# A transformer layer on one core: the order of helper work in its first stage is changed

## Time and profile before

| | before |
|---|---|
| median of three runs | 1362.12 us |
| the profiled execution | 1367.17 us |
| its span, first to last instruction | 1365.4 us |
| TensorE matmul busy | 1296.0 us, 95% |
| VectorE busy | 1061.4 us, 78% |
| ScalarE busy | 915.4 us, 67% |
| GpSimd busy | 959.2 us, 70% |
| mean granted TensorE clock | 0.988 |
| first stage | 0 to 310 us |

### The profile page before, as it was taken

How to read it: one execution, slowest core, us unless ns; L and a number is a source line. 1 busy time by engine, 2 the same in 40 slices (tenths; PEclk the granted TensorE clock), 3 DMA queues, 4 the chain that set the end, 5 groups by cost and what they waited for, 6 DMA issues and landing times.

```text
span 1365.4 us, 33237 instructions
## 1 busy us (share of the span) xinstructions
PE 1296.0 (95%) x11838; PEld 832.1 (61%) x11838; DVE 1061.4 (78%) x2856; ACT 915.4 (67%) x1752; POOL 959.2 (70%) x1304
## 2 busy tenths in 40 slices
PE   3899999998999999999999999999999999999988
PEld 2444444445666666676666767676767666666754
DVE  7767786887878778787878787878878787878753
ACT  3322322227878888787878788887878787878851
POOL 1322222206888888898888888898989888888853
PEclk9999999998999999999999999999999999999998
DMA  7489899543212121132323131322222232313121
GB/s 258 119 229 271 218 246 231 156 148 93 66 33 64 38 74 49 48 79 58 91 51 87 40 87 49 87 54 82 56 72 78 53 93 54 87 41 87 48 63 62
DMA packets 170870, 133.13 MB, mean 97 GB/s; under 512 B 81554, under 2 KB 139154, under 8 KB 170706
## 3 DMA queue, kind: packets, MB, share of 16 engines
q1 hardware_dynamic: 149042, 113.96, 31.2%
q10 hardware_dynamic: 21664, 17.05, 4.7%
HBM read 74.86 MB, written 42.21 MB: 86 GB/s over the span
## 4 chain that ended last, share of the span: by engine, by line
PE 64%; DVE 6%; ACT 3%; issue 2%; POOL 1%; DMA 0%; ACTq 0%; SPq 0%; DVEq 0%
PE bank L1344 20%; PE bank L1358 12%; PE bank L1322 9%; PE bank L179 8%; PE bank L1309 8%; PE bank L1375 6%; DVE ga L1246 1%; ACT th L1143 1%; DVE junk L202 1%; DVE mx L207 1%; ACT p L1166 1%; DVE probs L987 1%; POOL probs L987 1%; DVE fu L1251 1%; ACT probs L1136 1%
## 5 line engine op out<-in xcount | busy, mean ns | idle before, releaser
L1166 ACT ACTIVATE p<-bank,s_exp 128x512 f32<-128x512 f32 x576 | 395.8, 687 | 188.6 <-PE bank L1309 180.7
L987 POOL TENSOR_TENSOR probs<-p,probs 128x512 f16<-128x512 f32 x448 | 514.0, 1158 | 1.1 <-ACT probs L1136 1.1
L1136 ACT CAST probs<-p 128x512 f16<-128x512 f32 x576 | 351.8, 611 | 0.1
L1096 POOL TENSOR_SCALAR_AFFINE_SELECT p<-p 128x256 f32<-128x256 f32 (+1 forms) x320 | 152.8, 478 | 127.8 <-ACT p L1166 127.7
L207 DVE TENSOR_REDUCE mx<-bank 128x1 f32<-128x512 f32 x264 | 180.2, 686 | 74.7 <-PE bank L179 69.9
L179 PE MATMUL bank<-k_st,q_st 96*128 96x512 f16 (+3 forms) x792 | 221.6, 328 | 15.0 <-DVE mx L207 9.2
L1322 PEld LDWEIGHTS bank<-v_sb,probs 128*128 128x128 f16 x4608 | 198.1, 97 | 51.7 <-issue 1.6
L1309 PE MATMUL bank<-q_st,k_st 98*128 98x512 f16 (+3 forms) x768 | 221.2, 329 | 6.2 <-PEq L254 4.6
L1322 PE MATMUL bank<-v_sb,probs 128*128 128x65 f16 x4608 | 213.9, 192 | 2.7 <-DVE attn L1213 2.7
L1344 PE MATMUL bank<-xt,wg 128*128 128x256 f16 x1536 | 200.2, 273 | 6.3 <-DVE fu L1251 5.5
L1344 PE MATMUL bank<-xt,wu 128*128 128x256 f16 x1536 | 200.1, 273 | 0.0
(11 more groups left out here) (114 smaller groups left out, 1560.9 us busy)
## 6 DMA issues: line engine op xcount, KB each, us to landing
q_st<-q_parts SPq DMA_DIRECT2D x201, 64.0 KB, 2.1
k_st<-k_parts SPq DMA_DIRECT2D x201, 64.0 KB, 2.0
v_sb<-v_parts SPq DMA_DIRECT2D x66, 132.0 KB, 2.2
xt<-xn_parts SPq DMA_DIRECT2D x17, 512.0 KB, 4.5
v_parts<-res SPq DMA_DIRECT2D x8, 1056.0 KB, 6.7
xn_parts<-x_t SPq DMA_DIRECT2D x16, 512.0 KB, 7.7
q_parts<-qk_st SPq DMA_DIRECT2D x32, 256.0 KB, 4.5
k_parts<-qk_st SPq DMA_DIRECT2D x32, 256.0 KB, 4.2
```

The source lines that it names most:

```text
L987: ops.tensor_tensor(probs[s % 2][:, LO, at], p32[k % RING][:, :], probs[s % 2][:, HI, at], ALU.subtract).then_inc(signal, 1)
L1096: nc.gpsimd.affine_select(out=at, in_=at, compare_op=ALU.is_ge, fill=0.0, base=0, pattern=[[0, blocks], [1, P]], channel_multiplier=-1).th ...
L1136: nc.scalar.copy(probs[s % 2][:, HI, u * 512:(u + 1) * 512], p32[k % RING][:, :]).then_inc(p_hi, 1)
L1166: nc.scalar.activation(p32[k % RING][:, :], st_bank[(s + u) % 2][:, :], ACT.Exp, scale=s_exp[:, :]).then_inc(exp_done, 1)
```

## The change

- The bounds of weights 1 and 2: weight 1 is spread in bank 0 instead of 2, behind group 0 instead of ahead of it; weight 2's maximum is taken ahead of tile 0, its power right after the low part of weight 1, its spread behind group 2. Its high part is made after group 3 and it is copied at group 6. VectorE copies its pieces of weight 1 ahead of group 2.
- Statistics of x(t+2) are taken in tile t after group 10, and x(t+1) is normalised after group 0 of tile t; high part, load and transposes are two groups earlier.
- Loads and rounding of the ffn parts move to other slots, the heads' loads to the first group of tiles 3, 4 and 5.
- The bound of the ffn is spread after group 8 of tile 7, its maxima at group 4 and its factors at group 9.
- `xt` and the output buffers share memory with the first raw weight (`shared`), and SP loads the first `xt` at group 5 of tile 7. The constant rows of the fourth k buffer are set by GpSimd.

```diff
-WEIGHTS_SPLIT = {(0, 2): (2,), (3, 6): (3,)}
-WEIGHTS_COPIED = {(0, 3): (1,), (0, 5): (2,), (5, 8): (3,)}
-WMAX_SPREAD = {(0, 1): 2, (3, 3): 3}
-X_TURNED = {5: 0, 7: 1}
+WEIGHTS_SPLIT = {(0, 3): (2,), (3, 6): (3,)}
+WEIGHTS_COPIED_DVE = {(0, 2): (1,), (0, 6): (2,), (5, 8): (3,)}
+WEIGHTS_COPIED = {(0, 3): (1,), (0, 6): (2,), (5, 8): (3,)}
+WMAX_SPREAD = {(0, 0): 1, (0, 2): 2, (3, 3): 3}
+X_TURNED = {3: 0, 5: 1}
...
-FF_LOADED = {(1, 0): ((0, 1), (1, 1)),
-             **{(t, 6): ((2, t),) for t in range(1, NT - 1)},
-             **{(t, 8): ((0, t + 1),) for t in range(1, NT - 1)},
-             **{(t + 1, 0): ((1, t + 1),) for t in range(1, NT - 1)}, (NT - 1, 4): ((2, NT - 1),)}
-X_LOADED = {**{(t, 4): t + 2 for t in range(1, NT - 2)}, (0, 7): 2}
+FF_LOADED = {(1, 0): ((0, 1), (1, 1)), (1, 5): ((2, 1),), (1, 7): ((0, 2),), (1, 10): ((1, 2),), (2, 0): ((2, 2),),
+             **{(t, 6): ((0, t + 1),) for t in range(2, NT - 1)},
+             **{(t, 8): ((1, t + 1),) for t in range(2, NT - 1)},
+             **{(t + 1, 0): ((2, t + 1),) for t in range(2, NT - 1)}}
+X_LOADED = {**{(t, 2): t + 2 for t in range(1, NT - 2)}, (0, 7): 2}
...
-HEADS_LOADED = {(2, 3): 0, (2, 6): 1, (3, 3): 2}
+HEADS_LOADED = {(3, 0): 0, (4, 0): 1, (5, 0): 2}
...
+                    if (t, c) == (NT - 1, 5):
+
+                        sp.wait_ge(xt_stored, 16 * 2 * NT)
+                        sp.wait_ge(w_hi_done, 4)
+                        sp.wait_ge(w_lo_done, 4)
+                        sp.dma_start(keep["shared"][:, 0:KC * FT].bitcast(F16).rearrange("p (k t) -> p k t", t=FT),
+                                     xn_dram[0:1].rearrange("a p w k t -> p (a w k) t")).then_inc(keep["xt_loaded"], 16)
...
-            return bank[(2, 2, 5, 0)[m]][:, 0:P]
+            return bank[(2, 0, 5, 0)[m]][:, 0:P]
...
-                    if c == (7 if t == 0 else 4) and has_next(t):
+                    if c == (7 if t == 0 else 2) and has_next(t):
                         x_high(t + 1)
...
             weights_max(1)
             weights_power(1)
+            weights_max(2)
...
-            first_tile = {0: ("max 2",), 1: ("power 2",), 2: ("statistics",), 3: ("low 2",), 4: ("normalise",),
-                          6: ("magnitude 0",), 7: ("add 0",), 8: ("off 0", "magnitude 1"), 9: ("add 1",), 11: ("off 1",)}
-            last_tile = {0: ("magnitude 20", "add 20"), 1: ("off 20",), 2: ("magnitude 21",), 3: ("add 21",),
-                         4: ("off 21", "magnitude 22"), 5: ("add 22",), 6: ("off 22",), 7: ("magnitude 23", "add 23"),
-                         8: ("off 23",), 9: ("maxima",), 11: ("factors",)}
+            first_tile = {3: ("statistics 1",), 4: ("low 2",), 5: ("normalise 1",),
+                          6: ("magnitude 0",), 7: ("add 0",), 8: ("off 0", "magnitude 1"), 9: ("add 1",),
+                          11: ("off 1", "statistics 2")}
+            second_tile = {0: ("normalise 2",), 1: ("magnitude 2",), 2: ("add 2",), 3: ("off 2", "magnitude 3"),
+                           4: ("add 3",), 5: ("off 3",), 6: ("magnitude 4",), 7: ("add 4",), 8: ("off 4", "magnitude 5"),
+                           9: ("add 5",), 10: ("statistics 3",), 11: ("off 5",)}
+            last_tile = {0: ("magnitude 21", "add 21"), 1: ("off 21",), 2: ("magnitude 22",), 3: ("add 22",),
+                         4: ("off 22", "maxima"), 5: ("magnitude 23", "add 23"), 6: ("off 23",), 9: ("factors",)}
...
-                return {0: ("statistics",), 1: ("magnitude " + a,), 2: ("normalise",), 3: ("add " + a,),
+                later = (f"statistics {t + 2}",) if t + 2 < NT else ()
+                return {0: (f"normalise {t + 1}",), 1: ("magnitude " + a,), 3: ("add " + a,),
                         4: ("off " + a, "magnitude " + b), 5: ("add " + b,) + w3.get((t, 5), ()), 6: ("off " + b,),
                         7: ("magnitude " + c,), 8: ("add " + c,), 9: ("off " + c,),
-                        11: w3.get((t, 11), ())}
+                        10: later, 11: w3.get((t, 11), ())}
...
                     if t == c == 0:
                         weights_low(1)
+                        weights_power(2)
...
             turn_first_x()
-            spread_max(1)
...
-                    if t == 0 and c in (0, 3):
-
-                        pe.wait_ge(wpow_set, 2 + c // 3)
+                    if t == 0 and c == 3:
+
+                        pe.wait_ge(wpow_set, 3)
...
+                    if (t, c) == (NT - 1, 8):
+                        spread_ff_maxima()
...
-        xt = sb("xt", [P, 2, KC, FT], F16)
+        xt = keep["shared"][:, 0:KC * FT].bitcast(F16).rearrange("p (w k t) -> p w k t", w=2, k=KC)
...
-            load_tile(0)
...
+            nc.gpsimd.memset(k_st[3][3 * DK:3 * DK + 2, :], MSCALE).then_inc(ones_set, 1)
...
-            nc.vector.memset(k_st[3][3 * DK:3 * DK + 2, :], MSCALE).then_inc(ones_set, 1)
```

More of the change, by code:

```diff
@@ L259, in sem @@
             return ctx.enter_context(nc.semaphore(name))
-        w_raw = [sb(f"w_raw{m}", [P, KC, D], F32) for m in range(3)]
+        w_raw = [keep["shared"][:, :].rearrange("p (k d) -> p k d", k=KC)]
+        w_raw += [sb(f"w_raw{m}", [P, KC, D], F32) for m in (1, 2)]
         w_part = [sb(f"w_part{i}", [P, 2, KC, D], F16) for i in range(2)]
@@ L748, in plan_of @@
             def plan_of(t):
-                if t in (0, NT - 1):
-                    return last_tile if t else first_tile
-                a, b, c = (f"{3 * t - 1 + i}" for i in range(3))
+                if t in (0, 1, NT - 1):
+                    return {0: first_tile, 1: second_tile, NT - 1: last_tile}[t]
+                a, b, c = (f"{3 * t + i}" for i in range(3))
                 w3 = {(2, 11): ("max 3",), (3, 5): ("power 3",), (4, 11): ("low 3",)}
-                return {0: ("statistics",), 1: ("magnitude " + a,), 2: ("normalise",), 3: ("add " + a,),
+                later = (f"statistics {t + 2}",) if t + 2 < NT else ()
@@ L760, in tile @@
                 for c in range(12):
-                    for m in WEIGHTS_COPIED.get((t, c), ()):
+                    for m in WEIGHTS_COPIED_DVE.get((t, c), ()):
                         copy_weights(m)
@@ L793, in tile @@
                             take_step_off(int(m))
-                        elif has_next(t):
-                            {"statistics": norm_statistics, "normalise": normalise}[name](t + 1)
+                        elif name == "statistics":
+                            norm_statistics(int(m))
+                        elif name == "normalise":
+                            normalise(int(m))
                     if t >= NT - 2:
@@ L839, in spread_max, with spread_ff_maxima @@
                 nc.tensor.matmul(wmax_bank(m), ones[:, :], spread[:, m, :], start=True, stop=True).then_inc(wmax_mm, 1)
+            def spread_ff_maxima():
+                pe.wait_ge(rows.m_red, NM + (NM - 1) // len(early_banks) * len(early_banks) + 1)
+                pe.wait_ge(ffspread, 1)
+                nc.tensor.matmul(bank[0][:, :], ones[:, :], spread[:, :, :].rearrange("p n q -> p (n q)"), start=True,
+                                 stop=True).then_inc(ffmax_mm, 1)
             pe.wait_ge(ident_set, 1)
@@ L935, in attend @@
         res = keep["res"]
-        o_sb = [sb(f"o_sb{i}", [P, D], F32) for i in range(2)]
+        o_sb = [keep["shared"][:, KC * FT + i * D:KC * FT + (i + 1) * D] for i in range(2)]
         st_bank, m_bank = bank[0:2], bank[2:4]
@@ L943, in attend @@
         q_loaded, v_loaded, row_loaded, mt_copied = rows.q_loaded, rows.v_loaded, rows.row_loaded, rows.mt_copied
-        xt_loaded = sem("xt_loaded")
+        xt_loaded = keep["xt_loaded"]
         xb_loaded = sem("xb_loaded")
@@ L1068, in _ @@
             pool.sem_inc(res_done, 1)
+            nc.gpsimd.memset(k_st[3][3 * DK:3 * DK + 2, :], MSCALE).then_inc(ones_set, 1)
+            pool.wait_ge(ones_set, 1)
             def add_down(i, t):
@@ L1490, in build @@
                 "c_ff": sb("c_ff", [P, FC], F32), "ds_row": sb("ds_row", [P, D], F32),
-                "res": sb("res", [P, QB, D], F32), "v_stored": sem("v_stored")}
+                "res": sb("res", [P, QB, D], F32), "v_stored": sem("v_stored"),
+                "shared": sb("shared", [P, KC * D], F32), "xt_loaded": sem("xt_loaded")}
         rows = Rows()
```

## The result

The changed kernel takes 1352.76 us, the median of five runs (1350.97 to 1353.96), beside 1362.42 for the kernel before (five runs, 1360.91 to 1368.0): a ratio of 0.9918 (of the means), 95% interval 0.9895 to 0.9942. By the medians it is faster by 9.7 us, half of the 20 that were predicted, and outside the predicted range of 1336 to 1351. The profiled execution took 1353.43, with a span of 1351.7.

A forecast was written before the change was run, and what follows sets the result against it. The prediction took the first stage as the bound, with TensorE waiting for late x and losing clock. Terms 6.7 + 9.7 + 2.7 + 0.85 = 19.95 us took 1367.17 to 1347.2, or 1342 for the median; range 1336 to 1351.

The forecast's parts named there:

- Tile 5 is tighter ... Hidden, by 1.5 us: Tile 5: x's high part queues behind the scales' loads; even an 11.4 us landing, at T+31.5, precedes tile end T+33.0.
- The sign of being wrong that came true: First stage: the prediction is wrong if TensorE waits inside tiles for VectorE's low parts; no size given.
- Tile 0, 6.7 us: Tile 0's reordered weight bounds and statistics: tile 1 starts at 61.0 instead of 67.67, still set by x; 6.7 us.
- a rival at 1 to 2 us: VectorE's rounding delays x's low part 1 to 2 us per tile; sum 17 to 18 us instead of 20.
- Tiles 1 to 7, 9.7 us: x made a tile ahead: waits at tiles 3, 5 and 6 go, with half clock after two; 9.7 us.
- The end, 2.7 us: End of first stage: ffn maxima and factors earlier, so attention starts sooner after V's store; 2.7 us (2.3 to 2.9).
- The first x, 0.85 us: Start of attention: its first x is loaded some 20 us sooner, in tile 7, so TensorE's wait goes; 0.85 us.
- slower: Attention's 3072 matmuls at L1344 read x from shared memory; at 10 ns more each, 1373 us; chance 0.03.
- Clock kept: Tile 1 and start of attention: clock stays full after shorter gaps, 1.6 + 3 us more, 1337 us; chance 0.10.
- Some waits for x stay: Tile 6 and one more keep 2 to 3 us waits and half clock, 6 to 8 us back, 1349; chance 0.15.
- faster by over 0.5%: Whole kernel: more than 6.8 us faster, covering the forecast, kept clock, staying waits and half of "little"; chance 0.93.

The follow-up runs named there:

- b: Changed kernel with the scales' loads issued ahead of the x load after group 2 of tile 5; 1349.89 us.
- c: Changed kernel with the loads of head 2 at the start of tile 6 instead of tile 5; 1352.35 us.
- e: Changed kernel with the high part of tile 6's x made after group 3 of tile 5 instead of group 2; 1352.15 us.
- a: Changed kernel with the scales' loads issued after group 4 of tile 6 instead of group 2 of tile 5; 1347.7 us.
- n: Kernel h with tile 0's order of weights, statistics and normalising as before the change; 1349.25 us.
- h: Kernel a with tile 0's high part of the next x after group 6 instead of 7, its transpose ahead of group 7's store; 1344.21 us.
- g: Kernel a leaving out the rounding of the first two ffn weight parts, but for 8 columns of one step; 1344.08 us in one run.
- d: The kernel before the change, unedited, profiled a second time; 1361.73 us.
- f: The kernel before with only the heads' loads moved to the start of tiles 3, 4 and 5; 1357.6 us.
- i: Kernel h with ffn maxima and factors at their old groups and attention's first x loaded in attention; 1346.92 us.
- k: Kernel h with x's load, high part and transposes at their old groups, statistics and heads' loads left as changed; 1354.59 us.

## Why the prediction was wrong

The step that failed is "Tile 5 is tighter ... Hidden, by 1.5 us". Its first error is a length. With T the tile's start (188.68), it took the scales' issues at their old length behind 0.4 us of x load, so ScalarE would be free at about T+12.3; it was free at T+19.3 (207.99 - 188.68). Of the 7.0 us, 1.9 are the x load's wait for the normalising, which the prediction had itself at T+9.5 and did not put ahead of the load, and 5.1 are the issues, 9.05 us instead of 3.91 with 1 MB before them in the queue. b and c show that it was the x load's place and not the head's loads.

The second error is the path. The prediction followed x's chain alone behind the issues: queued behind the same issues, and behind the high part of x, was the emptying of group 3, which TensorE wanted first. The prediction had named this rule itself, for VectorE (four banks, 2.8 us of cover), and not applied it to ScalarE. With the length that it assumed this would have cost nothing: the high part ends at T+14.3, emptying and low part of group 3 (0.6 and 0.7) at T+15.6, and group 7 wants the bank at T+18.1 (seven groups of 2.59). With the real length it became a wait, 1.9 us of which are the high part's place by run e. Cost: 4.37 us of wait and 2.4 of half clock in the profile, 4 to 5 us by the medians. Without it (run a) the time, 1347.7, lies within the predicted range. The sign of being wrong that came true is the last one named, TensorE waiting inside a tile for VectorE's low part.

The Trainium skill, "DMA: Bandwidth & Descriptors", section "Issuing engines are not separate DMA queues", says that the time a sequencer spends to initiate a DMA is usually small beside the DMA. Here it was not: 5.25 us of issue, for 256 KB that had landed 8.5 us after the issue began.

The other steps:

- *Tile 0, 6.7 us.* Right in mechanism, too large: tile 1 starts 5.0 us sooner from profile to profile (67.67 to 62.63; 68.92 in the second profile of before), and by 5.3 from n to h. The wait for the bound and the half clock of group 0 went, but group 0 started at 23.08, not 22.2 (x's own transposes took 3.11 us instead of 2.41, and 0.83 of waiting followed), and x's low part took 6.69 us, not 5.6. The prediction priced such a block by VectorE as a rival at 1 to 2 us; g, with most of VectorE's steps beside it gone, makes it 1.46 shorter. But the steps alone do not set the price: in the changed kernel the low part took 6.69, 6.25 and 5.54 us in tiles 0, 2 and 3, each time beside the same two steps (1.8 and 1.31 us), which began 0.6, 1.6 and 2.7 us after it. Nor are the steps new beside it, as the prediction has it: in the old order it took 6.5 to 6.6 us beside such steps in tiles 1 to 5. The rule of the Trainium skill, "SBUF — State Buffer", section "Who interferes with whom", fits these numbers; no run here has the low part with no two-input step beside it.
- *Tiles 1 to 7, 9.7 us.* The waits at 3, 5 and 6 went; without the new wait (run a), from tile 1's start to attention's first matmul took 229.3 us, against 243.1 and 240.6 in the two profiles of before. That is 11.3 to 13.9, where the two terms, x's slots and the end, made 12.4. But 3.3 us of the 9.7 were in the first profile only (tile 6, run d). f shows 3.5 us of it to be the heads' move alone. One term was put at nothing without a reason: the issue of the first transposing DMA, which held SyncE for 4.7, 8.0, 4.5 and 4.1 us in tiles 1 to 4. In tiles 2 to 4 the second was issued at T+21.2 to T+22.6, not T+17.3, and in tile 2 the spare time was all but gone, as the last section shows.
- *The end, 2.7 us.* The gap fell from 4.56 to 2.53, 2.0 us: the start came 1.14 after the store of V, not 0.55.
- *The first x, 0.85 us.* No wait for it is left. But that wait differs from run to run in the old order (0.85, 1.23 in run d, 0.50 in f), and i, with the load in attention, waited only 0.34 and was, 15 score matmuls in, 0.5 us further on than h, counted from attention's start: the granted clock was back at 1.00 some 6.5 us after that start in i and 8.4 in h. In sum with the end, i is 0.7 to 2.7 us slower than h, not clear of noise.
- *The base.* One profiled execution was taken for the kernel. By the second one the tile starts held 6.8 us and not 9.7 (3.59 + 1.7 + 0.44 + 1.03), and 2.6 us of attention were the first's alone; the shift to the median could not set the first right, since the gain was subtracted whole. From the first profile to that of the changed kernel, attention's start moved by 11.7 us (310.81 to 299.13), where 19.1 were forecast for it. The 7.4 that are missing are 6.7 (tile 5), 1.7 (tile 0) and 0.7 (the end), less 1.7 gained that was not forecast: 1.0 at the row maxima in tile 6, for which TensorE waited 1.18 us in three places before and 0.17 after, and 0.7 that was not traced.
- *Two readings.* The one slice of the page below full that is not the last is the tenth, 307 to 341 us: it is the gap between the stages and the start of attention, and no slice of the first stage shows the lost clock. And the chances given for "faster by over 0.5%" add up to 0.94, not 0.93.

Of the rivals, "slower" found nothing: the matmuls that read `xt` from shared memory take 272 to 273 ns each, 272 before. "Clock kept" did not come true in the changed kernel (2.85 us of wait at tile 1) but does in g and h, at 1.41 and 1.29. "Some waits for x stay" named a time, 1349, that is nearer to the measured one than the forecast, but not for its reason: in the changed kernel's profile no tile from 2 to 7 starts late.

What stays open: why single transposes take 13 to 15 us to land, and whether that is why runs of one kernel differ by 3 us and more.

## What to carry to other kernels

Before a transfer's issue is moved, write down everything behind it on the engine that issues it, and take its length from what will stand ahead of it in the queue, not from the old trace. A wait seen in one profile is worth its length only if a second profile has it too. And slack put before a DMA should be counted against the longest landing seen and from when its queue is really free: here 2.4 us were left over the longest landing (T+28.7 against T+31.1), and 0.1 us remained of them in tile 2, since the DMA was issued 5.3 us later than forecast.

## What the runs showed of the hardware

The same transposing DMA landed after 4.2 to 15.0 us. In the first profile of the kernel before, two of whose landings are in the earlier trace rows, 12 of 14 took 4.2 to 6.8 us; in the changed kernel tile 2's took 11.9 and 8.4, and the last landed at 126.4, when tile 3 started at 126.46. A shorter distance to x's load alone does not explain it: in tile 2 that load was issued 4.9 us before the first transpose, 6.0 in the kernel before, but 7.1 in k's tile 1, where they took 12.4 and 15.0.

TensorE's granted clock stayed at 1.00, which is 2.4 GHz, after waits of 1.29, 1.41, 1.63 (n, tile 6) and 1.68 us. At 2.2 us it went both ways: 0.50, which is 1.2 GHz, in the 3 us after the 2.21 of run d, but 1.00 after the 2.22 in run f, at the same place:

```profile
67.88 20.88 PE L876 MATMUL bank<-x_t,w_t 128*128 128x512 f16 x96 [2.22 <-issue]
```
